# GpSimd's arithmetic of the main part moved to VectorE, and b_out added to a DRAM copy of x

## What is computed

```python
xn = _layernorm(x)
x = x + gnn(xn, W, b, src, dst) + mix(xn[None], w_qkv, w_out, b_out)[0]
x = x + ffn(_layernorm(x)[None], gate_w, gate_b, w1, b1, w2, b2)[0]

def gnn(x, W, b, src, dst):                      # N = 6250
    h = x * rsqrt(max(deg_out, 1))[:, None]
    agg = segment_sum(h[src], dst, N)
    h = relu((agg * rsqrt(max(deg_in, 1))[:, None]) @ W + b)
    return h / max(norm(h, axis=1), 1e-12)

def mix(x, w_qkv, w_out, b_out):                 # 8 heads of 64
    q, k, v = heads(x @ w_qkv.T); k, v = instance_norm(k), instance_norm(v)
    return (q @ (k.T @ v) / N) @ w_out.T + b_out

def ffn(h, ...):                                 # top-1 of 8 experts, capacity 977, hidden 1024
    y = relu(buf @ w1 + b1) @ w2 + b2            # rows beyond the capacity give nothing
    return y_of_token * prob
```

## Time and profile before

| | us |
|---|---|
| median of 3 runs | 1470.52 |
| lowest and highest run | 1468.57, 1472.99 |
| profiled execution, first to last instruction | 1429.1 |
| TensorE busy | 1337.7 (94%) |
| VectorE busy | 1248.9 (87%) |
| ScalarE busy | 962.9 (67%) |
| GpSimd busy | 648.8 (45%) |

### The profile page before, as it was taken

The page is one execution under the profiler, slowest core; times in us unless marked ns, Lnnn a source line. Parts: engine busy times, 40 slices in busy tenths (PEclk is TensorE's granted clock), DMA queues, the critical chain, the costliest instruction groups (busy, mean ns, idle before and its releaser), DMA issues. The chain is left out here.

```text
span 1429.1 us, 43152 instructions
## 1 busy us (share of the span) xinstructions
PE 1337.7 (94%) x14715; PEld 1128.4 (79%) x14717; DVE 1248.9 (87%) x2315; ACT 962.9 (67%) x2239; POOL 648.8 (45%) x645
## 2 busy tenths in 40 slices
PE   4899999958999999999999999999998999899987
PEld 3466666637899999999999999999995788889986
DVE  7899999988789999999999999999976586867786
ACT  5588888775567767677677677676663658464754
POOL 4557663062234433334433344333331676776574
PEclk9899999988999999999999999999999999999999
DMA  9211111000011111121111121111113443353220
GB/s 299 60 42 46 54 45 39 23 31 1 4 62 50 37 37 37 37 72 38 37 37 37 37 73 37 37 37 37 41 71 104 129 139 107 102 161 95 76 77 26
DMA packets 61264, 89.57 MB, mean 63 GB/s; under 512 B 10231, under 2 KB 40591, under 8 KB 61154
## 3 DMA queue, kind: packets, MB, share of 16 engines
q1 hardware_dynamic: 50032, 67.20, 13.9%
q0 software_dynamic: 11136, 21.23, 5.3%
HBM read 62.91 MB, written 34.49 MB: 68 GB/s over the span
## 5 line engine op out<-in xcount | busy, mean ns | idle before, releaser
L1621 PE MATMUL bank<-reg_b,reg_a 128*128 128x256 f16 x4802 | 642.7, 273 | 0.7 <-ACT reg_a L1206 0.7
L1206 ACT ACTIVATE reg_a<-bank 128x392 f16<-128x392 f32 x784 | 358.8, 499 | 159.2 <-PE bank L1613 154.3
L1621 PEld LDWEIGHTS bank<-reg_b,reg_a 128*128 128x128 f16 x4802 | 428.9, 97 | 42.7 <-issue 0.9
L1860 DVE TENSOR_TENSOR reg_c<-iota_v,reg_c 128x2048 f16<-128x2048 f16 (+1 forms) x298 | 432.2, 1465 | 21.6 <-PE bank L1613 11.2
L845 POOL COPY key_deg<-deg_k 128x1 f32 (+1 forms) x49 | 105.0, 2143 | 463.0 <-DVE reg_c L1989 463.0
L1613 PE MATMUL bank<-reg_a,reg_c 128*128 128x98 f16 x3136 | 261.4, 208 | 6.1 <-DVE reg_e L2069 2.2
L1613 PEld LDWEIGHTS bank<-reg_a,reg_c 128*128 128x128 f16 x3136 | 213.5, 98 | 24.9 <-issue 7.9
L1860 DVE TENSOR_TENSOR reg_a<-iota_h,reg_c 128x1568 f16<-128x1568 f16 x196 | 215.7, 1101 | 0.0
L1816 PE MATMUL bank<-w_hi,hid_hi 128*128 128x256 f32 (+1 forms) x368 | 107.3, 292 | 12.7 <-DVE w_lo L2342 7.5
L1818 PE MATMUL bank<-w_hi,hid_lo 128*128 128x256 f32 (+1 forms) x368 | 104.6, 284 | 0.0
L1817 PE MATMUL bank<-w_lo,hid_hi 128*128 128x256 f32 (+1 forms) x368 | 104.5, 284 | 0.0
(11 more groups left out here) (360 smaller groups left out, 2529.4 us busy)
## 6 DMA issues: line engine op xcount, KB each, us to landing
reg_b<-in_L_ffn_w SPq DMA_DIRECT2D x16, 1024.0 KB
tok_rows<-reg_e SPq DMA_DIRECT2D x24, 512.0 KB, 3.8
x_t<-in_x SPq DMA_DIRECT2D x24, 256.0 KB
xnT_t<-xnT_rows SPq DMA_DIRECT2D x24, 256.0 KB, 2.9
out<-reg_e SPq DMA_DIRECT2D x24, 256.0 KB
xnT_rows<-xnT_t SPq DMA_DIRECT2D x13, 256.0 KB, 2.0
reg_a<-in_x SPq DMA_DIRECT2D x1, 3072.0 KB, 24.1
xnT_rows<-mix_hl SPq DMA_DIRECT2D x12, 256.0 KB, 2.0
```

The source lines that it names most:

```text
L1206: return a.activation(AT[k].rearrange("p h (w t) -> p h w t", w=2)[:, :, :, s * GROUP:(s + 1) * GROUP], tile_ps[bk][:, 0:GROUP * 2 * NB].r ...
L1621: ins = t_.matmul(agg_ps[k][:, 0:D], AT[k][:, h, :], h_all[:, h, half * D:(half + 1) * D], start=(first and h + half == 0), stop=(last and ...
L1860: return v_.tensor_tensor(out.rearrange("p t (v u) -> p t v u", u=2), iota.rearrange("p (v u) -> p v u", u=2).unsqueeze(1).to_broadcast(sh ...
```

## The change

- VectorE makes the keys whole: `keys(b, k)` takes the place of `key_halves`, with the rest of GpSimd's `block_keys` as one fused operation (slot number times 256 minus the degree term, maximum with the source's low part) and a copy of the high part. It waits for TensorE's transposition of the buffer's last keys (`key_ready`).
- VectorE reads the sum out of PSUM itself: `scaled(b, k)` multiplies by 1/sqrt(deg_in) and the column norms in one operation, per block; `biased(q)` adds `gnn_b_bc` per pair. ScalarE's `agg_evac` and GpSimd's `first` are gone.
- x is copied within DRAM to `x_bias` by one DMA on SP's queue, behind the load of wq and ahead of the small loads and the first `store_kv`; a second one writes b_out five times in a row to `b_out_rows`. GpSimd adds b_out in ten DMAs that accumulate, each over 625 rows in 125 descriptors of five rows, one in each of the pairs 3 to 12 of `pace()`, ahead of that pair's gathers. SP waits for all ten before `load_pair(0)`, and all later loads of x rows read `x_bias`.
- GpSimd keeps `h_part`, now in one piece, and the rounds of nodes with more than 64 edges.

The diff, cut to its core:

```diff
@@ -105,6 +105,11 @@
...
 XB = 6
+XB_ROWS = 250
+XB_JOIN = 5
+XB_PARTS = 10
+XB_FROM = 3
+assert N % (XB_JOIN * XB_PARTS) == 0 and XB_JOIN * D <= 2048
@@ -125,6 +130,7 @@
...
     tok_rows = dram("tok_rows", (NPAD, TOKW))
+    x_bias, b_out_rows = dram("x_bias", (N, D)), dram("b_out_rows", (XB_JOIN, D))
@@ -616,6 +619,9 @@
...
         sp.dma_start(wq[:, :, :], wv[:, 0:IC, :]).then_inc(w_in2, 16)
+        sp.dma_start(x_bias.rearrange("(p j) d -> p (j d)", p=XB_ROWS), x.rearrange("(p j) d -> p (j d)", p=XB_ROWS)
+                     ).then_inc(xb_in, 16)
+        sp.dma_start(b_out_rows, b_out.rearrange("(a d) -> a d", a=1).to_broadcast([XB_JOIN, D])).then_inc(xb_in, 16)
         sp.dma_start(gate_w_sb[:, :, :], gate_w.rearrange("(c p) d -> p c d", p=P)).then_inc(w_in2, 16)
@@ -624,7 +630,7 @@
...
             if blocks_of(q) == 1:
-                n = LAST if rows is x or rows is out else P
+                n = LAST if rows is x_bias or rows is out else P
             rows = rows[ds(first, n), :]
@@ -641,7 +647,7 @@
...
         def load_pair(q):
-            sp.dma_start(x_t[:, :, :], pair_rows(x, q)).then_inc(x_ld, 16)
+            sp.dma_start(x_t[:, :, :], pair_rows(x_bias, q)).then_inc(x_ld, 16)
             sp.dma_start(xnT_t[:, :, :, :].rearrange("p l m d -> p (l m d)"), xnT_rows[ds(q * P, P), :]
@@ -658,14 +664,15 @@
...
         sp.wait_ge(hw_ready, NB)
+        sp.wait_ge(xb_set, 16 * XB_PARTS)
         load_pair(0)
...
         sp.wait_ge(agg_done, NB - 1)
-        sp.dma_start(last_fin.x[0:LAST, 0, :], pair_rows(x, NQ)).then_inc(x_ld, 16)
-        sp.dma_start(last_fin.x[LAST:P, 0, :], x[0:P - LAST, :]).then_inc(x_ld, 16)
+        sp.dma_start(last_fin.x[0:LAST, 0, :], pair_rows(x_bias, NQ)).then_inc(x_ld, 16)
+        sp.dma_start(last_fin.x[LAST:P, 0, :], x_bias[0:P - LAST, :]).then_inc(x_ld, 16)
         last_T = xnT_rows[NQ * P:(NQ + 1) * P, :].rearrange("p (l m d) -> p l m d", l=2, m=2)
@@ -772,11 +779,21 @@
...
+        def bias_rows(n):
+            if n == 0:
+                pool.wait_ge(xb_in, 32)
+            rows = N // XB_PARTS
+            part = x_bias[n * rows:(n + 1) * rows, :].rearrange("(p j) d -> p (j d)", j=XB_JOIN)
+            b_rows = b_out_rows.rearrange("(a j) d -> a (j d)", a=1).to_broadcast([rows // XB_JOIN, XB_JOIN * D])
+            g.dma_start(part, b_rows, accum_op=ALU.add).then_inc(xb_set, 16)
...
                 pool.wait_ge(hot_used, HBUF + HFIRST + HBUF - 1 + HBUF * q)
+            if i == 0 and XB_FROM <= q < XB_FROM + XB_PARTS:
+                bias_rows(q - XB_FROM)
             if i == G_FIRST:
@@ -839,19 +856,6 @@
...
-        def block_keys(b, k):
-            pool.wait_ge(key_int, b + 1)
-            apart(pool)
-            g.tensor_copy(key_deg[:, :], deg_k[:, ds(b, 1)])
-            g.tensor_copy(key_t[k][:, :, :], key_i).then_inc(key_mask, 1)
-            pool.wait_ge(key_mask, b * 2 + 1)
-            apart(pool)
-            g.tensor_scalar(key_off[:, :], iota_k[:, :], key_deg[:, :], 0.0, ALU.subtract, ALU.max).then_inc(key_mask, 1)
-            pool.wait_ge(key_mask, b * 2 + 2)
-            apart(pool)
-            g.tensor_tensor(key_t[k][:, 0, :], key_t[k][:, 0, :], key_off, ALU.add).then_inc(key_set, 1)
         def h_part(tiles):
@@ -861,53 +865,20 @@
...
-        pool.wait_ge(degin_set, 3)
-        block_keys(0, 0)
         pool.wait_ge(deg_ok, 1)
         pool.wait_ge(hw_out, H_POOL[-1] + 1)
-        h_part(H_POOL[:6])
-        block_keys(1, 1)
-        h_part(H_POOL[6:])
+        h_part(H_POOL)
         pool.wait_ge(end_ready, 1)
...
         def gnn(b, k, fin, with_rounds=True):
-            fin(0)
-            if not fixed(b, NB - 1) and not fixed(b, NB - 2):
-                pool.wait_ge(key_ready, b + 1)
-                apart(pool)
-                block_keys(b + 2, k)
-            if not fixed(b, 0):
-                more(b - 1, rounds_of(pool, b - 1) if with_rounds else None)
-        def first(q):
-            w = blocks_of(q)
-            pool.wait_ge(x_ld, (NQ + 2) * 16 if fixed(q, NQ) else (q + 1) * 16)
-            xt = fin_of(q).x[:, 0:w, :]
-            g.tensor_tensor(xt, xt, b_out_bc[:, :].unsqueeze(1).to_broadcast([P, w, D]), ALU.add).then_inc(x_added, 1)
-            if fixed(q, NQ):
-                return
-            if not first_pair(q):
-                pool.wait_ge(fin_relu, q)
-            pool.wait_ge(agg_out, q * 2 + (w + 2))
-            apart(pool)
-            gs = fin_of(q).g[:, 0:w, :]
-            g.tensor_tensor(gs, fin_of(q).agg[:, 0:w, :], norm_bc[:, :].unsqueeze(1).to_broadcast([P, w, D]), ALU.mult
-                            ).then_inc(fin_pool, 1)
-            pool.wait_ge(fin_pool, q + 1)
-            apart(pool)
-            g.tensor_tensor(gs, gs, gnn_b_bc[:, :].unsqueeze(1).to_broadcast([P, w, D]), ALU.add
-                            ).then_inc(fin_scaled, 2)
+            if with_rounds and not fixed(b, 0):
+                more(b - 1, rounds_of(pool, b - 1))
         def tail():
-            last_rounds = rounds_of(pool, NB - 1)
-            first(NQ - 1)
-            first(NQ)
-            more(NB - 1, last_rounds)
-        pool.wait_ge(b_in, 48)
-        main_phase(pool, gnn, lambda b, s: None, lambda q, s: first(q), lambda q, s: None, tail)
+            more(NB - 1, rounds_of(pool, NB - 1))
+        main_phase(pool, gnn, lambda b, s: None, lambda q, s: None, lambda q, s: None, tail)
@@ -1206,14 +1177,6 @@
...
-        def agg_evac(b, k):
-            if not fixed(b, 0) and not fixed(b, 1) and not fixed(b, NB - 1):
-                act.wait_ge(fin_scaled, b - k)
-            act.wait_ge(agg_done, b + 1)
-            apart(act)
-            agg = last_fin.agg if fixed(b, NB - 1) else agg_s
-            a.activation(agg[:, k, :], agg_ps[k][:, 0:D], ACT.Copy, scale=rin[:, ds(b, 1)]).then_inc(agg_out, 1)
         def more(b, k, rounds):
@@ -1231,8 +1194,6 @@
...
                 act.wait_ge(deg_ok, 2)
-            if not fixed(b, 0) and not fixed(b, 1):
-                agg_evac(b - 2, k)
             for s in range(SLOTS):
@@ -1301,13 +1262,11 @@
...
             last_rounds = rounds_of(act, NB - 1)
-            agg_evac(NB - 2, 1)
             for s in (8, 9, 11):
...
             more(NB - 1, 0, last_rounds)
-            agg_evac(NB - 1, 0)
             for s in (8, 9):
@@ -1982,11 +1941,15 @@
...
-        def key_halves(b):
+        def keys(b, k):
             apart(dve)
...
             v_.tensor_scalar(key_i[:, 1, :], src_b, 7, None, ALU.logical_shift_right).then_inc(key_int, 1)
+            dve.wait_ge(key_int, b + 1)
+            apart(dve)
+            v_.scalar_tensor_tensor(key_t[k][:, 0, :], iota_k[:, :], deg_k[:, ds(b, 1)], key_i[:, 0, :], ALU.subtract, ALU.max)
+            v_.tensor_copy(key_t[k][:, 1, :], key_i[:, 1, :]).then_inc(key_set, 1)
@@ -2016,9 +1979,10 @@
...
             dve.wait_ge(slots_in, 16 * NB)
-            key_halves(0)
             dve.wait_ge(base_set, 4)
             dve.wait_ge(consts, 20)
+            dve.wait_ge(degin_set, 3)
+            keys(0, 0)
             dve.wait_ge(deg_ok, 1)
@@ -2043,8 +2007,7 @@
...
                 rounds()
-                dve.wait_ge(key_set, 1)
-                key_halves(1)
+                keys(1, 1)
             if q < NQ:
@@ -2114,11 +2077,25 @@
...
                 if c == 1 and not fixed(b, NB - 1) and not fixed(b, NB - 2):
-                    dve.wait_ge(key_set, b + 2)
-                    key_halves(b + 2)
+                    dve.wait_ge(key_ready, b + 1)
+                    keys(b + 2, k)
                 fin(c)
...
                 more(b - 1, rounds_of(dve, b - 1) if with_rounds else None)
+        def scaled(b, k):
+            out_ = last_fin.g[:, 0, :] if fixed(b, NB - 1) else g_s[:, k, :]
+            dve.wait_ge(agg_done, b + 1)
+            apart(dve)
+            v_.scalar_tensor_tensor(out_, agg_ps[k][:, 0:D], rin[:, ds(b, 1)], norm_bc[:, :], ALU.mult, ALU.mult
+                                    ).then_inc(agg_out, 1)
+        def biased(q):
+            w, gs = blocks_of(q), fin_of(q).g
+            dve.wait_ge(agg_out, q * 2 + (w + 2))
+            apart(dve)
+            v_.tensor_tensor(gs[:, 0:w, :], gs[:, 0:w, :], gnn_b_bc[:, :].unsqueeze(1).to_broadcast([P, w, D]), ALU.add
+                             ).then_inc(fin_scaled, 2)
@@ -2131,6 +2108,8 @@
...
         def prepare(b, c):
+            if (b, c) == (2, 0):
+                scaled(0, 0)
             if (b, c) == (1, 1):
@@ -2150,7 +2129,10 @@
...
             w, o = blocks_of(q), fin_of(q)
+            if c == 0:
+                scaled(q * 2 + 1, 1)
             if c == 1:
+                biased(q)
                 n[0] = 0
@@ -2186,19 +2168,16 @@
...
                                   mix_bc[:, 0:D].unsqueeze(1).to_broadcast([P, w, D]), ALU.mult), q)
-            dve.wait_ge(x_added, q + 1)
+            dve.wait_ge(x_ld, (NQ + 2) * 16 if fixed(q, NQ) else (q + 1) * 16)
```

(15 more changed lines are left out.)

17 lines of the change are left out of this document (7 added, 10 removed).

## The result

| | before | after |
|---|---|---|
| median, us | 1469.55 (4 runs, 1467.98 to 1472.99) | 1487.18 (4 runs, 1483.75 to 1490.68) |
| ratio after to before | | 1.0105, 95% interval 1.0079 to 1.0131 |
| profiled execution, span | 1429.1 | 1482.6 |

The account below looks back on a forecast made before the run. TensorE's list of work was taken to bound the main loop, unchanged; passage +0.2, tail -0.5 and copy +2.5 gave +2.2 us: span 1431.3, with 41.4 outside 1472.7 us. Range 1468.5 to 1486, the forecast's own 1470 to 1477.

Parts of the forecast that it names:

- TensorE's list of work bounds the loop, VectorE's slack covers the rest: Main loop: ends when TensorE's work ends; new VectorE waits, covered by masks 11 us ahead, cost nothing.
- VectorE's own balance: Main loop: VectorE gains 2.6 us of work a pair, saves 3.2, and gets 0.6 us emptier.
- GpSimd beside VectorE: Main loop: GpSimd's wide operations swell VectorE's masks by 3.2 us a pair, which vanishes with the change.
- The passage: From k/v phase into main loop: longer keys, less contention, no wait for GpSimd's keys; +0.2 us, bounds -1.2 to +0.8.
- The tail: Behind the last block: VectorE takes over work but loses swelling from GpSimd; -0.5 us, bounds -1.2 to +0.5.
- The copy: Start of k/v phase: a 15 us copy of x delays the first store; +2.5 us, bounds 0 to +8.4.
- Later pairs can't catch up: k/v phase: later pairs run at a steady 10.5 us, so the copy's delay at the start remains.
- 41.4 us lie outside the span: Whole kernel: 41.4 us between the 1429.1 us span and the 1470.52 us median, taken as unchanged.
- Rival A: Start: the copy runs on fewer DMA engines; 1486 us with a copy of 27 us; chance 0.22.
- Rival B: k/v phase: slow accumulations, at 12 us each outlasting the cover, +20 us, 1493 us; chance 0.08.
- C: Start: the copy delays nothing, as the store passes it or it stays at 11 us; 1470.2 us; chance 0.12.
- D: Passage and tail: VectorE's relief reaches the time, 5 us faster, 1465.5 us; chance 0.08.

Follow-up runs that it names:

- best: Changed kernel without the copy and accumulating DMAs, GpSimd adding b_out in SBUF, VectorE's order as in keys_late: 1473.48 us, ratio 1.0019.
- keys_late: Changed kernel with scaled() moved behind the normalization and the even blocks' keys behind the low part on VectorE: 1467.03 us, ratio 0.9990.
- second profile of before: The kernel before, unchanged, profiled once more: 1466.01 us, span 1464.8.
- dram_only: Kernel before with only the copy of x and the accumulating DMAs; all arithmetic but the x add stays on GpSimd: 1473.33 us, ratio 1.0030.
- before_copies: Kernel before with ten 640 KB copies of x in pairs 2 to 11, result never read: 1472.28 us, ratio 1.0047.

## Why the prediction was right or wrong

The forecast was 1472.7 us and "no change"; the kernel is at 1487.2, 1 us above the top of the range, and slower. The share of 0.43 for slower rested on the copy and the accumulations, not on what happened. That the two times are only 1% apart speaks for no part of the mechanism: the term that made the result stood at nothing.

- **"TensorE's list of work bounds the loop, VectorE's slack covers the rest": wrong, and this is the step that failed.** Busy time (TensorE at work for 200.00 of 200 us, VectorE for 191.23) and the list of waits were read rightly. But I took the cover from the masks (11 us ahead) and applied it to everything in VectorE's queue. The finishing steps have no such cover: the low part of the rows had 0.06 us. I costed the new waits and the insertion ahead of this chain at nothing; they cost 0.79 us a pair (31.25 - 30.46), 16.2 us over the loop.
- **VectorE's own balance: right, and of no use.** Masks are at 1.22 and 0.97 us throughout, GpSimd is at 0.00 of 200 us, VectorE's work for a pair falls from 191.16 / 200 x 30.46 = 29.1 us to 180.50 / 200 x 31.25 = 28.2 us, by 0.9 where I had 0.6. What is new in a set of keys took 0.84 - 0.20 = 0.64 us (I had 0.54), scaled() 0.48 (0.42). The sign of VectorE's load says nothing of its order.
- **GpSimd beside VectorE.** With GpSimd silent the masks are at their short times, 1.22 and 0.97 us where they took 2.03 to 2.31 beside GpSimd's operations, and in best one wide operation of GpSimd makes a VectorE operation last 1.29 us in place of 0.18. But the 3.2 us a pair that I read as swelling, 77 us over 24 pairs, did not come as a saving; the 0.47 us a pair between keys_late and best are the nearest measure of what GpSimd's silence is worth where VectorE's chain has no slack.
- **The passage (+0.2): off, and on the other side.** I gave 0.6 us for TensorE's wait for GpSimd's keys. In the second profile of before it is 3.7 us in two waits, behind a one-element copy of GpSimd that took 5.94 us among VectorE's masks (waits of TensorE, 318 to 425 us, then GpSimd's timeline):

```profile
PE bank L1559 <- POOL reg_c L852: 3.7, 2, 2.8
...
PE bank L1581 <- DVE more_r L1996: 1.4, 1, 1.4
```

```profile
368.88 5.94 POOL L845 COPY key_deg<-deg_k 128x1 f32<-128x1 f32 x1 [17.86 <-DVE reg_c L1989]
```

  The same stretch of the first profile has two such waits too, of 1.5 us in all; the window of rows 3 begins behind the first of them. In the changed kernel the first wait is gone. The one for the round counts, which I had seen growing by 1.0 us, grew from 1.4 to 4.2 us, but other work covers part of that: the passage takes 70.6 us, 3.1 us less than in the second profile of before and 1.2 us less than in the first.
- **The tail (-0.5): not told apart.** Tail and experts took 343.4 us after and 345.1 before; other profiles of kernels with the same work there run from 342.9 to 347.9.
- **The copy (+2.5): mis-sized.** I took 15 us out of 11.1 to 18.6. The packets' own time is 128 x 2.3 / 16 = 18.4 us, the upper end, but from the first to the last of them it was 22.8 us (34.7 to 57.6), with small loads in between, and the store's own packets ran from 57.3 to 61.4 us. ScalarE got the store at 61.77 us, 11.1 us later than before (50.69), not 3.8. The rows of ScalarE and of SP's issue of the store, changed kernel:

```profile
61.77 0.60 ACT L1033 ACTIVATE mix_hl<-bank 128x512 f16<-128x512 f32 x1 [10.70 <-DMA xnT_rows<-xnT_t]
```

```profile
35.29 0.43 SPq L639 DMA_DIRECT2D xnT_rows<-xnT_t  x1
```

  26.5 us after its issue, where I had 21. The cost at the eleventh histogram is 7.7 us, inside the bound of 8.4. The +2.5 and that bound also hold 0.6 and up to 3 us for a slower clock and for VectorE's later masks, a term that no run shows by itself. What the runs show in its place: the granted clock is at 0.50 to 0.52 from 57 to 66 us in the changed kernel, behind TensorE's wait of 10.28 us for ScalarE, and 64 matmuls of the histogram take 2.82 us there (62.96), where 32 take 0.87 us at 1.00 (69.65); in the first profile of before it is at 0.50 from 57 to 60 us only, and at 0.96 and 1.00 in the next two stretches of 3 us.
- **"Later pairs can't catch up": wrong.** That rested on the steady 10.5 us of a profile whose k/v phase was not that of the timed runs. In the second profile of before the pairs behind the start take 10.5 to 21 us, in the changed kernel 10.5 to 15. The changed kernel is 6.4 us behind at the last histogram.
- **"41.4 us lie outside the span": wrong.** 1.2 us do. The gap between span and median was a sign that the profiled execution was not a typical one, and I should have priced the k/v phase by that. It did not touch the loop's term, since the loop was the same in both; the k/v terms rested on it.
- **Rival A** (0.22 of the forecast's shares), a copy that runs on fewer of the DMA engines, is out; no run shows a copy that does. Its 128 packets of 2.3 us each, in 22.8 us, kept 12.9 engines busy on the average, and with the loads beside them 0.96 of 16 were busy from 30 to 60 us. The packets were of 50,000 bytes with 250 rows as with 1250.
- **Rival B** is out: 4.8 us for the one I took the packets of, inside my 1.9 to 5.6. By the HBM counts of the pages ten of them add 6.41 MB read and 6.40 MB written (dram_only 75.72 and 47.29 MB, before_copies 69.31 and 40.89): one stream of 640 KB read by each, where I had counted two. **C** is out: the copy delays the start. **D** is half right: VectorE's relief does reach the time in the passage (1.2 to 3.1 us), but the loop takes more than it gives.

## What to carry to other kernels

A list of waits without an entry says that nobody waited, not that there was room. For each instruction that is moved or added in an engine's queue, measure the slack of every consumer behind it, from the end of the operand to the start of its use, not only that of the largest one. Where two engines pass work back and forth, moving work to an engine with time to spare can still lengthen the chain (here by 0.79 us a pair); put new work behind the step that the other engine needs next. Keep large copies out of the queue in front of a transfer that has a due time, or cut them into several and spread them: here the copy in one piece had the eleventh histogram at 79.8 us and in ten parts, on GpSimd's queue, at 71.1. And when the span of a profile is 3% under the timed runs, take another profile before costing anything from it.
